# Joint block products for six shared chunks of batches 0 and 1, and the mixed weights of both batches on GpSimd

## The chip, the cores and the metric

The kernel runs on one core of a Trainium2 chip. The metric is the device time of one execution in microseconds. Engine names in the profile: PE is TensorE's matmul side and PEld its weight load, DVE is VectorE, ACT is ScalarE, POOL is GpSimd, SP is the engine that issues most DMAs.

## The reference

Four layers follow one another, each added to its input, for x of 4 batches x 512 rows x 256 columns, all in fp32:

```
x = x + shared_mlp(x) + sum over the 2 best of 8 experts of share * skill_mlp(x)   # gelu(x@gate) * (x@up) @ down, inner width 1024
x = x + (silu(x@Wu.T + bu) * (x@Wg.T + bg)) @ Wd.T + bd                            # one expert of 8, inner width 512
x = x + x @ (sum_g y[b,g] * weight[g] * mask).T + bias                             # mixed weights, 256 x 256
x = x + x @ W_base.T + b_base + 2 * lora(x)                                        # low rank, mixed by y[b]
```

The experts of the first two layers and the shares y[b] come from `cond_8`, one row for each batch. The shared MLP of the first layer is the same for all batches, the skill MLPs are chosen for each batch.

## The kernel before

Inner width is worked off in chunks of 128. The first layer has 8 shared chunks and 2 x 8 skill chunks for each batch, the second has 4. A chunk is: gate and up products (12 matmuls of 512 columns), gelu on ScalarE into `hid`, the product with up on VectorE (`hidden`, L966 to L970), and a down product (6 matmuls). Each fp32 operand is split into a high half (fp32r, made by ScalarE: `hid_hi`, `w_hi`) and a low half (the rest, made by VectorE: `hidden_lo` L976, `split` L956), and each product is three matmuls: high x high, high x low, low x high. The weights of two chunks come as one piece of four DMAs into one of three `raw` slots; SP issues them in a fixed order and waits for the splits of the piece three earlier.

Every engine's order is written out by hand. TensorE interleaves: gate and up of chunk i, then down of chunk i-1. VectorE in a chunk does `hidden`, the low half of the weights of chunk i+2 (`split`), `hidden_lo`, and then what the tables at the top of the file name for this chunk: turning x or the second layer's weights, summing `a2` (the mixed weights of the third layer, 8 steps of `a2_step_n`, L1022 to L1031), bias sums (`bias_base`, L1202 to L1207), residual sums.

Batches 0 and 1 run one after the other through `batch`, 24 chunks each, the 8 shared ones first. Batches 2 and 3 share their 8 shared chunks: `pair_head` does 8 skill chunks of batch 2, then 8 calls of `pair_unit` do one skill chunk of batch 2 and one shared chunk of both batches, then `pair_rest` does batch 3's 16 skill chunks. In a unit the gate and up of the shared chunk, for two batches, would be 8 block products of three matmuls; seven are done, on sums of the x blocks (`t_tiles`, made once) and sums of the weight blocks (`pair_sums` L1374 to L1379, `pair_main_lo` L1386, `pair_sums_lo` L1391), and their results are put together by VectorE (L1405, L1418, L1431) and ScalarE copies. TensorE's products 0 to 6 of a unit are lines L1825 to L1827; the second waits for the last sum (L1431) of the unit before, the down product after it for `hidden_lo` (L976) of the unit's own skill chunk.

At the start, TensorE turns batch 0's x and sums the routing result (`route`, L1787); VectorE's `take_route` (L1157, L1160) writes the chosen experts, for which SP waits before any skill piece. Pieces 1 and 2 are of the shared MLP and are issued before that wait.

Of the kernel before, what the change touches and what calls it, by code (L numbers as in the profile page):

```python
# [5 lines left out]
F32 = mybir.dt.float32  # L6
# [9 lines left out]
E = 8  # L16
# [6 lines left out]
CH = 3 * MLP_CHUNKS  # L23
C1 = H1 // P
PIECES = CH // 2
# [10 lines left out]
MINE_AT = 3  # L36
X_TURN_AT = {4: 1, 7: 2, 9: 3}
X_HI_AT = {5: 1, 8: 2, 10: 3}
X_LO_AT = {6: 1, 9: 2, 12: 3}
L3_TURN_AT = 6  # L40
L3_OPERAND_AT = 7
L3_HI_AT = 8
BIAS_BASE_AT = 1
BIAS_LORA_AT = 2
BIAS_AT = 3
BIAS_LOADS_AT = 18
L3_LO_AT = 10
L1_AFTER = 5
X2_AT = L1_AFTER + 1
OUT_AT = 8  # L50
C_AT = 13
CA_AT = CH - 1
XSUM_AT = 14
TURN_AT = 15
# [3 lines left out]
C_PLACE = {2: 1, 3: 3}  # L58
OUT_PLACE = {2: 7}
X2_SUM = {2: 5}  # L60
# [3 lines left out]
CA_PLACE = 13  # L64
A_HEAD = {1: (0, 1), 2: (2, 3), 3: (4, 5), 4: (7,), 6: (8,), 7: (9,)}
A_BESIDE_L1 = 6
PAIR_SUMS_AT = 4
PAIR_SUMS_LO_AT = 5
X1_PLACE = 2
# [7 lines left out]
def first(b):  # L77
    return isinstance(b, int) and b == 0

def a_steps_at(b, i):  # L80

    if not first(b):
        return (i - 9,) if 9 <= i <= E + 10 else ()
    return {13: (0,), 14: (1, 2)}.get(i, (i - 12,) if 15 <= i <= E + 13 else ())

def a_split_at(b):
    return E + 14 if first(b) else E + 11

PAIR = 2
SKILL = 2 * MLP_CHUNKS  # L90
L1_PLACE = {1: 5, 2: 3, 3: SKILL}
X2_PLACE = {2: 4}
HIDDENS = [0, CH, 2 * CH + C1, 2 * CH + SKILL + 2 * C1, 2 * CH + 2 * SKILL + 2 * C1]
PAIR_FROM = HIDDENS[PAIR] + MLP_CHUNKS + C1
PAIR_TO = HIDDENS[PAIR + 1]
PRODUCTS, COPIES, SUMS, PARTS = 7, 3, 4, 3
# [5 lines left out]

def tile_of(g):
    return g % 2 if g < PAIR_FROM else 1 if g < PAIR_TO else (g + 1) % 2


def same_tile_before(g):

    return g - 1 if PAIR_FROM <= g <= PAIR_TO else g - 2


def splits_done(b, i):
    return min(b, PAIR) * (CH - 2) + (2 + (b - PAIR) * SKILL if b >= PAIR else 0) + i + 1

# [4 lines left out]

def tails_before(b):  # L120
    return b * 3 - 1 + len(PREPS) if not first(b) else len(PREPS)


def hidden_of(b, i):
    return i + (0 if first(b) or i <= L1_PLACE[b] else C1)


def turned(i):
    c, odd = divmod(i - TURN_AT, 2)
    return c if 0 <= c < C1 and not odd else None  # L130
# [6 lines left out]
def product_of(b, what):  # L137
    order = ("c", "ca", "out") if b > PAIR else ("c", "out", "ca") if b == PAIR else ("out", "c", "ca")
    return order.index(what) + 1 - first(b)


def raw_slot(p):
    return (p - 1) % RAW_SLOTS if p else RAW_SLOTS - 1


def raw_uses(b, p):

    s = raw_slot(p)
    per = sum(raw_slot(q) == s for q in range(1, PIECES))
    return per * b + sum(raw_slot(q) == s for q in range(1, p + 1))  # L150


PAIR_PIECES = [("skill", 0), ("skill", 2), ("skill", 4), ("pair", 0), ("skill", 6), ("skill", 8), ("pair", 2), ("skill", 10),
               ("pair", 4), ("skill", 12), ("pair", 6), ("skill", 14)] + [("skill", SKILL + c) for c in range(0, SKILL, 2)]


def pair_raw_slot(j):
    return (j + 2) % RAW_SLOTS


def pair_raw_uses(j):
    return raw_uses(1, (9, 10, 11)[j % RAW_SLOTS]) + j // RAW_SLOTS + 1


X_LAST = 4 * PAIR + KD


def piece_of(kind, c):
    return PAIR_PIECES.index((kind, c - c % 2))


def build(nc, t):
    ctx = ExitStack()
    with ctx:
# [3 lines left out]
        def sem(name):  # L178
# [54 lines left out]
        base_nat = sums[:, :, :].rearrange("p (k n) m -> p k (n m)", k=KD)  # L233
# [10 lines left out]
                    3: xs[:, :, :].rearrange("p k s -> p (k s)")}  # L244
# [93 lines left out]
        a2_step = sem("a2_step")  # L338
        weights_f = sem("weights_f")
# [61 lines left out]
        t_tiles = (out_pair[:, 0], sums_flat, c3[:, :], out_pair[:, 1])  # L401
# [22 lines left out]
        PHASE = [(res_hi, res_lo, n) for n in range(2)] + [(w_hi, w_lo, n) for n in range(2, W_SLOTS)]  # L424
        AFTER_PAIR = [(res_hi, res_lo, 0), (w_hi, w_lo, 0)] + [(w_hi, w_lo, 2), (w_hi, w_lo, 3), (res_hi, res_lo, 0), (res_hi, res_lo, 1)] * 4

        def split_slots(i, b=0):
# [5 lines left out]
            if i < 2:  # L433
                return res_hi[:, i], res_lo[:, i]
# [1539 lines left out]
```

## Time and profile before

| | us |
|---|---|
| time, median of 3 runs (483.36 to 483.56) | 483.42 |
| span of the profiled execution | 481.8 |
| PE busy | 477.8 |
| DVE busy | 374.9 |
| ACT busy | 262.7 |
| POOL busy | 33.7 |

The page gives the profiled execution's own time as its span, from the first to the last instruction. The timed runs last 1.6 us longer than the span. Busy times are unions of instruction intervals; those of PE contain its weight waits within the pipeline, so a pace is better read from the distance of two starts.

### The profile page before, as it was taken

To read this page: it belongs to the slowest core of one execution; us is meant where nothing else is said; L and a number is where in the kernel's file an instruction comes from. 1 tells how busy PE (TensorE), PEld (TensorE's weight loads), DVE (VectorE), ACT (ScalarE), POOL (GpSimd) and SP (SyncE) were. 2 spreads that over 40 slices of the span, in tenths; PEclk is the share of its full clock that TensorE was granted. 3 is DMA by queue.
4 is the path that set the end of the run, shared out by engine and by line. 5 is a ranking of instruction groups with operands and counts; after the bars stand their busy time and mean duration, and the time that the engine had idled before them with its cause. 6 is when DMAs were issued, how large, how long until landed. Compare 5 with 4: busy or idle time off the path is not lost.

```text
span 481.8 us, 6729 instructions
## 1 busy us (share of the span) xinstructions
PE 477.8 (99%) x2184; PEld 398.5 (83%) x2184; DVE 374.9 (78%) x642; ACT 262.7 (55%) x418; POOL 33.7 (7%) x56
## 2 busy tenths in 40 slices
PE   9999999999999999999999999999999999999997
PEld 7888888888888888888888888888888888888886
DVE  7678989969536578985988988998887799965465
ACT  5556555545446344555547566676765365544432
POOL 1910302000100200000000020000000100000000
PEclk9999999999999999999999999999999999999999
DMA  7988985386230532424290053404059224000002
GB/s 224 199 184 201 261 168 153 71 195 134 70 106 0 136 106 67 131 67 131 78 180 4 2 149 93 131 1 131 0 117 205 74 66 128 4 1 0 2 0 87
DMA packets 114538, 48.90 MB, mean 101 GB/s; under 512 B 66552, under 2 KB 113272, under 8 KB 114504
## 3 DMA queue, kind: packets, MB, share of 16 engines
q1 hardware_dynamic: 111360, 42.88, 35.9%
q0 software_dynamic: 2560, 5.21, 4.5%
q10 hardware_dynamic: 584, 0.39, 0.3%
q8 instruction: 17, 0.28, 0.3%
q14 instruction: 17, 0.14, 0.1%
HBM read 46.36 MB, written 2.10 MB: 101 GB/s over the span
## 4 chain that ended last, share of the span: by engine, by line
PE 99%; DVE 0%; DVEq 0%; issue 0%
PE bank_a L1568 9%; PE bank_a L1569 9%; PE bank_b L1569 9%; PE bank_a L1570 9%; PE bank_b L1570 9%; PE bank_b L1568 9%; PE out L1593 6%; PE out L1596 6%; PE out L1592 6%; PE tail L1593 2%; PE tail L1596 2%; PE tail L1592 2%; PE tail L1570 2%; PE tail L1569 2%; PE tail L1568 2%; PE bank_a L1825 2%
## 5 line engine op out<-in xcount | busy, mean ns | idle before, releaser
L706 ACT ACTIVATE hid_hi<-hid 128x512 fp32r<-128x512 f32 x96 | 60.7, 632 | 93.2 <-DVE hid L968 54.0
L976 DVE TENSOR_TENSOR hid_lo<-hid,hid_hi 128x512 fp32r<-128x512 f32 x96 | 66.0, 687 | 16.8 <-ACT hid_hi L706 16.8
L698 ACT ACTIVATE hid<-bank_a 128x512 f32<-128x512 f32 x80 | 47.7, 596 | 55.1 <-PE bank_a L1570 54.3
L968 DVE SCALAR_TENSOR_TENSOR hid<-bank_b,mine,hid 128x512 f32<-128x512 f32 x64 | 47.7, 746 | 32.8 <-PE bank_b L1570 30.6
L956 DVE TENSOR_TENSOR w_lo<-raw,w_hi 128x768 fp32r<-128x768 f32 x57 | 54.1, 949 | 0.4 <-ACT w_hi L665 0.4
L1568 PE MATMUL bank_a<-x_hi,w_hi 128*128 128x512 f32 x114 | 44.5, 391 | 0.0
L1569 PE MATMUL bank_a<-x_lo,w_hi 128*128 128x512 f32 x114 | 44.5, 390 | 0.0
L1570 PE MATMUL bank_a<-x_hi,w_lo 128*128 128x512 f32 x114 | 44.4, 390 | 0.0
L1570 PE MATMUL bank_b<-x_hi,w_lo 128*128 128x512 f32 x114 | 44.4, 389 | 0.0
L1569 PE MATMUL bank_b<-x_lo,w_hi 128*128 128x512 f32 x114 | 44.4, 389 | 0.0
L1568 PE MATMUL bank_b<-x_hi,w_hi 128*128 128x512 f32 x114 | 44.4, 389 | 0.0
L1593 PE MATMUL out<-hid_hi,w_lo 128*128 128x512 f32 x104 | 40.5, 389 | 0.0
L1592 PE MATMUL out<-hid_hi,w_hi 128*128 128x512 f32 x104 | 40.5, 389 | 0.0
L665 ACT ACTIVATE w_hi<-raw 128x768 fp32r<-128x768 f32 x44 | 36.9, 838 | 0.2 <-DMA raw<-in_L_cond_shared_down 0.2
L1596 PE MATMUL out<-hid_lo,w_hi 128*128 128x512 f32 x104 | 32.0, 389 | 0.0
L1568 PEld LDWEIGHTS bank_a<-x_hi,w_hi 128*128 128x128 f32 x114 | 21.4, 188 | 4.5 <-DVE w_lo L956 0.2
L1568 PEld LDWEIGHTS bank_b<-x_hi,w_hi 128*128 128x128 f32 x114 | 21.4, 188 | 4.5
L1570 PEld LDWEIGHTS bank_a<-x_hi,w_lo 128*128 128x128 f32 x114 | 21.4, 188 | 4.5
L1569 PEld LDWEIGHTS bank_b<-x_lo,w_hi 128*128 128x128 f32 x114 | 21.4, 188 | 4.4
L1570 PEld LDWEIGHTS bank_b<-x_hi,w_lo 128*128 128x128 f32 x114 | 21.4, 188 | 4.4
L1569 PEld LDWEIGHTS bank_a<-x_lo,w_hi 128*128 128x128 f32 x114 | 21.4, 188 | 4.2
L1593 PEld LDWEIGHTS out<-hid_hi,w_lo 128*128 128x128 f32 x104 | 19.5, 188 | 4.0
(346 smaller groups left out, 1108.9 us busy)
## 6 DMA issues: line engine op xcount, KB each, us to landing
raw<-in_L_cond_skill_gate SPq DMA_DIRECT2D x32, 256.0 KB, 3.0
raw<-in_L_cond_skill_up SPq DMA_DIRECT2D x32, 256.0 KB, 3.2
raw<-in_L_cond_skill_down SPq DMA_DIRECT2D x64, 128.0 KB, 3.3
raw<-in_L_cond_shared_down SPq DMA_DIRECT2D x22, 128.0 KB, 3.8
raw<-in_L_cond_shared_gate SPq DMA_DIRECT2D x10, 256.0 KB, 3.6
raw<-in_L_cond_shared_up SPq DMA_DIRECT2D x10, 256.0 KB, 3.7
raw_gate<-in_L_cond_W_gate SPq DMA_DIRECT2D x16, 128.0 KB, 3.0
early<-in_L_cond_weight POOLq DMA_DIRECT2D x2, 1024.0 KB, 7.6
```

Of the source, the lines that this page charges most:

```text
L665: nc.scalar.activation(split_slots(i)[0], raw[:, raw_slot(p), :, (i % 2) * P:(i % 2 + 1) * P], ACT.Copy).then_inc(split_hi, 1)
L698: nc.scalar.activation(hid[:, tile_of(g)], bank_a[tile_of(g)][:, :], func, **kw).then_inc(act_ready, 1)
L706: nc.scalar.activation(hid_hi[:, tile_of(g)], hid[:, tile_of(g)], ACT.Copy).then_inc(hid_hi_ready, 1)
L956: nc.vector.tensor_tensor(lo, raw[:, slot, :, (i % 2) * P:(i % 2 + 1) * P], hi.bitcast(F32), ALU.subtract).then_inc(split_lo, 1)
L968: ins = nc.vector.scalar_tensor_tensor(tile, bank, weight, tile, ALU.mult, ALU.mult)
L976: nc.vector.tensor_tensor(hid_lo[:, tile], hid[:, tile], hid_hi[:, tile].bitcast(F32), ALU.subtract).then_inc(hid_lo_ready, 1)
L1568: nc.tensor.matmul(out, w_hi_, v_hi, start=start, stop=False)
L1569: nc.tensor.matmul(out, w_hi_, v_lo, start=False, stop=False)
L1570: return nc.tensor.matmul(out, w_lo_, v_hi, start=False, stop=stop)
L1592: nc.tensor.matmul(banks[:, j, :], hi[:, 4 + j], hid_hi[:, tile], start=start, stop=False)
L1593: nc.tensor.matmul(banks[:, j, :], lo[:, 4 + j], hid_hi[:, tile], start=False, stop=False)
L1596: ins = nc.tensor.matmul(banks[:, j, :], hi[:, 4 + j], hid_lo[:, tile], start=False, stop=stop)
```

## The change

Batches 0 and 1 get the joint stage that 2 and 3 have, for six of the eight shared chunks. Each of the two now starts with 2 shared chunks of its own (`SHARED`). `first_head` does 12 chunks of batch 0 (2 shared, 10 skill), six units do the last 6 skill chunks of batch 0 beside six joint chunks, `second` does 18 chunks of batch 1 with the second layer's four chunks after chunk 4. The functions of the joint stage take the batch as an argument; banks and tiles of batch 0's units are those with number 0.

Beside that:
- The piece after the first one is a skill piece; SP waits for `chosen_ready` ahead of it. `take_route` is cut in two: `take_chosen` is done right after the first part of the first weights, `take_picks` where `take_route` stood.
- x of batches 2 and 3 is loaded and turned in batch 1 instead of batch 0; combined x tiles of batches 0 and 1 are made in chunks 5 to 10 of batch 0.
- The `a2` steps of batches 0 and 1 are done by GpSimd (`first_a2`), in its queue between DMAs; the first waits for `bias_base`, which VectorE now does in unit 0. Those of batches 2 and 3 stay on VectorE.
- The second layer's weights of batch 0 are turned in units 1 to 4, those of batch 1 in its chunks 13 to 16, one chunk each time.
- Placement tables of bias sums, c3 and ca products follow. Sums of batch b go to bank `out0` or `tail` by the parity of b.

```diff
-L1_PLACE = {1: 5, 2: 3, 3: SKILL}
+PAIRED = {0: 0, 2: 6}
+SHARED = 2
+OWN = (SHARED + 2 * MLP_CHUNKS, SHARED + 2 * MLP_CHUNKS, 2 * MLP_CHUNKS, 2 * MLP_CHUNKS)
+UNITS = {b: MLP_CHUNKS - c for b, c in FIRST_JOINT.items()}
+L1_PLACE = {1: 4, 2: 3, 3: OWN[3]}
+T_AT = {5: 0, 7: 1, 9: 2, 10: 3}
+MAIN_AT = 10
+SUMS_AT = {0: 10, 2: 4}
+SUMS_LO_AT = {0: 11, 2: 5}
-PAIR_TURN = {1: 0, 2: 1, 4: 2, 6: 3}
-PAIR_TURN_AT = {2: 0, 3: 1, 5: 2, 7: 3}
+PAIR_TURN = {0: {1: 0, 2: 1, 3: 2, 4: 3}, 2: {1: 0, 2: 1, 4: 2, 6: 3}}
+PAIR_TURN_AT = {0: {2: 0, 3: 1, 4: 2, 5: 3}, 2: {2: 0, 3: 1, 5: 2, 7: 3}}
+PIECE_ORDER = ([("own", 0, c) for c in range(0, 14, 2)] + [("joint", 0, 2), ("own", 0, 14), ("joint", 0, 4), ("own", 0, 16), ("joint", 0, 6)]
...
 # SP
-            load_piece(1, None, *shared)
-            load_piece(2, None, *shared)
-            load_piece(3, splits_done(0, 1), *shared)
-            load_x(1)
             sp.wait_ge(chosen_ready, 1)
+            for j, (kind, b, c) in enumerate(PIECE_ORDER):
...
 # GpSimd
+            def first_a2(b):
+                if b == 0:
+                    pool.wait_ge(base_sums, KD)
+                    pool.wait_ge(w2_in, 48)
+                    pool.wait_ge(tail_free, len(PREPS))
+                else:
+                    pool.wait_ge(weights_lo, 3 * b - 1)
+                nc.gpsimd.tensor_scalar(a2[:, :], w2_raw[:, 0, :], picks[:, b, 5:6], None, ALU.mult).then_inc(a2_step, 1)
+                for n in range(1, E):
+                    pool.wait_ge(a2_step, b * A_STEPS + n)
+                    nc.gpsimd.tensor_scalar(share, w2_raw[:, n, :], picks[:, b, 5 + n:6 + n], None, ALU.mult).then_inc(a2_share, 1)
+                    pool.wait_ge(a2_share, b * (E - 1) + n)
+                    nc.gpsimd.tensor_tensor(a2[:, :], a2[:, :], share, ALU.add).then_inc(a2_step, 1)
+                pool.wait_ge(a2_step, b * A_STEPS + E)
+                nc.gpsimd.tensor_tensor(a2[:, :], a2[:, :], mask_nat[:, :], ALU.mult).then_inc(a2_step, 1)
...
 # VectorE, first_head (12 chunks of batch 0)
+                    hidden(0, i, weight=mine[:, skill_of(0, i):skill_of(0, i) + 1] if i >= SHARED else None)
+                    if i + SPLIT_AHEAD <= UNIT_AT[0]:
+                        split(0, i + SPLIT_AHEAD)
+                    if i:
+                        hidden_lo(0, i)
...
+                    if i == SUMS_AT[0]:
+                        pair_sums(0, 0)
+                    if i == MAIN_AT + 1:
+                        pair_main_lo(0, 0)
+                    if i == SUMS_LO_AT[0]:
+                        pair_sums_lo(0, 0)
+                    if i == C_PLACE[0] + 2:
+                        weights_split_lo(0, 1, c3_hi, c3_lo, c3[:, :])
 # VectorE, pair_unit(b, m)
+                if m in PAIR_TURN[b]:
+                    turn_chunk(b, PAIR_TURN[b][m])
+                if unit == 0:
+                    bias_base()
+                hidden(b, n, weight=mine[:, 1:2])
 # VectorE, start
             first_parts(0)
+            take_chosen()
             first_x_parts(0)
...
 # TensorE
+            first_head()
+            for m in range(UNITS[0]):
+                pair_unit(0, m)
+            second()
             pair_head()
-            for m in range(MLP_CHUNKS):
-                pair_unit(m)
+            for m in range(UNITS[JOINT]):
+                pair_unit(JOINT, m)
```

## Rows read from the trace of the kernel before

**Rows 1.** Page, part 1: busy us, share of the span, instructions.
```profile
PE 477.8 (99%) x2184; PEld 398.5 (83%) x2184; DVE 374.9 (78%) x642; ACT 262.7 (55%) x418; POOL 33.7 (7%) x56
```
**Rows 2.** Page, part 4: chain that ended last, by engine.
```profile
PE 99%; DVE 0%; DVEq 0%; issue 0%
```
**Rows 3.** Chain in order of time (start us, us, what): low-half down matmuls.
```profile
21.25 0.45 PE out L1596 x2
...
57.97 0.45 PE out L1596 x2
...
103.59 0.45 PE out L1596 x2
```
**Rows 4.** Engines by stretch, one unit: length; busy us (instructions) by engine; clock, DMA.
```profile
287.90:299.46 11.56, 11.56 (x53) 9.59 (x52) 10.52 (x22) 7.75 (x14) 0.00 (x0) 1.00 0.42 130
```
**Rows 5.** Timeline at the start (start us, us, engine, line, instruction, idle before).
```profile
6.04 0.42 DVE L1534 TENSOR_TENSOR res_lo<-raw,res_hi 128x256 fp32r<-128x256 f32 x1
...
9.51 0.15 DVE L1157 CAST chosen<-out 1x12 int32<-1x12 f32 x1
...
11.35 0.85 ACT L665 ACTIVATE w_hi<-raw 128x768 fp32r<-128x768 f32 x1 [0.23 <-DMA raw<-in_L_cond_shared_down]
...
12.23 0.96 DVE L956 TENSOR_TENSOR w_lo<-raw,w_hi 128x768 fp32r<-128x768 f32 x1 [0.38 <-ACT w_hi L665]
...
13.24 0.19 PEld L1568 LDWEIGHTS bank_a<-x_hi,w_hi 128*128 128x128 f32 x1 [0.24 <-DVE w_lo L956]
```
**Rows 6.** Timeline of SP's DMA issues.
```profile
13.31 5.40 SPq L482 DMA_DIRECT2D early<-in_x  x4
20.01 0.43 SPq L448 DMA_DIRECT2D raw<-in_L_cond_skill_gate  x1
...
37.16 0.52 SPq L448 DMA_DIRECT2D raw<-in_L_cond_skill_gate  x1
...
38.38 1.39 SPq L451 DMA_DIRECT2D raw<-in_L_cond_skill_down  x2
```
**Rows 7.** Page, part 6: DMA issues, KB each, us to landing.
```profile
raw<-in_L_cond_skill_gate SPq DMA_DIRECT2D x32, 256.0 KB, 3.0
...
raw<-in_L_cond_skill_down SPq DMA_DIRECT2D x64, 128.0 KB, 3.3
```
**Rows 8.** Timeline of DVE in a chunk that has no weight split.
```profile
103.16 0.75 DVE L968 SCALAR_TENSOR_TENSOR hid<-bank_b,mine,hid 128x512 f32<-128x512 f32 x1 [0.71 <-PE bank_b L1570]
104.61 0.69 DVE L976 TENSOR_TENSOR hid_lo<-hid,hid_hi 128x512 fp32r<-128x512 f32 x1 [0.70 <-ACT hid_hi L706]
```
**Rows 9.** Groups of instructions (count, busy us, mean ns): low halves of a unit's weight blocks.
```profile
L1386 DVE TENSOR_TENSOR w_lo<-raw,w_hi 128x512 fp32r<-128x512 f32 x8 | 5.5, 686 | 0.3 <-ACT w_hi L756 0.3
```
**Rows 10.** Timeline of PE, unit 0 and the start of unit 1.
```profile
283.48 0.40 PE L1827 MATMUL bank_a<-x_hi,w_lo 128*128 128x512 f32 x1
...
288.60 0.40 PE L1825 MATMUL bank_b<-x_hi,w_hi 128*128 128x512 f32 x1
...
290.19 0.62 PE L1596 MATMUL out<-hid_lo,res_hi 128*128 128x512 f32 x2
```
**Rows 11.** Timeline of DVE in units 0 and 3.
```profile
283.92 0.69 DVE L1418 TENSOR_TENSOR xs<-bank_a,xs 128x512 f32<-128x512 f32 x1 [0.81 <-PE bank_a L1827]
...
286.67 0.69 DVE L1431 TENSOR_TENSOR xs<-bank_b,xs 128x512 f32<-128x512 f32 x1
...
288.48 0.68 DVE L976 TENSOR_TENSOR hid_lo<-hid,hid_hi 128x512 fp32r<-128x512 f32 x1
...
317.39 0.69 DVE L1418 TENSOR_TENSOR xs<-bank_a,xs 128x512 f32<-128x512 f32 x1 [0.41 <-PE bank_a L1827]
```
**Rows 12.** Timeline of DVE, bias sums in batch 1.
```profile
115.82 0.42 DVE L1202 CUSTOM_DVE_ANT_0 bias_all<-sums,bias_all 128x256 f32<-128x256 f32 x1
...
117.14 0.69 DVE L970 TENSOR_TENSOR hid<-bank_b,hid 128x512 f32<-128x512 f32 x1
```
**Rows 13.** Timeline of POOL: the only arithmetic that reads SBUF there.
```profile
1.32 0.28 POOL L581 TENSOR_SCALAR_AFFINE_SELECT ident<-ident 128x128 f32<-128x128 f32 x1 [0.23 <-POOL ident L579]
```

More of the change, by code:

```diff
@@ L554, in later_skill @@
[L554 to L565 removed]
+            sp.wait_ge(chosen_ready, 1)
@@ new lines, in _ @@
+            for j, (kind, b, c) in enumerate(PIECE_ORDER):
+                if j == 0:
+                    continue
+                own_skill = c - (SHARED if b < JOINT else 0)
+                if kind == "own" and own_skill >= 0 and own_skill % MLP_CHUNKS == 0:
+                    rows = skill_rows(b, own_skill // MLP_CHUNKS)
+                load_piece(j, *(rows if kind == "own" and own_skill >= 0 else shared))
+                if (kind, b, c) == ("own", 0, 4):
+                    load_x(1)
+                if (kind, b, c) == ("own", 0, 14):
+                    for n in range(3):
+                        first_l1(n)
+                if (kind, b, c) == ("own", 1, 2):
+                    sp.wait_ge(turn_f, 3 * C1)
+                    load_x(2)
+                    load_x(3)
+                if (kind, b, c) in (("own", 1, 12), ("own", 2, 6), ("own", 3, 2)):
+                    later_l1(b)
@@ L655, in split @@
             def split(b, i):
-                if b >= PAIR:
-                    return later_split(b, i)
-                p = i // 2
-                act.wait_ge(raw_in[raw_slot(p)], 64 * raw_uses(b, p))
-                if i - W_SLOTS >= 2:
-                    wait(act, down_done, hiddens_before(b) + hidden_of(b, i - W_SLOTS) + 1)
-                elif not first(b):
-                    last = max(c for c in range(CH) if c >= 2 and (c - i) % W_SLOTS == 0)
-                    act.wait_ge(down_done, hiddens_before(b) - CH + last + 1)
@@ L729, in l1_chunks, with combined_hi @@
                     hidden_hi(b, n0 + c)
-                    if b == PAIR:
+                    if b == 1 and c == 2:
+                        later_x_hi(2)
+                    if b == JOINT:
                         beside_l1(c)
+            def combined_hi(b, which):
+                steps = 5 * (b // JOINT)
+                for n, step in which:
+                    act.wait_ge(t_step, steps + step)
+                    nc.scalar.activation(combined(b, x_hi, n), t_tiles[b][n], ACT.Copy).then_inc(t_hi, 1)
@@ new lines, in pair_unit @@
+                if not last:
+                    pair_main_hi(b, m + 1)
+                else:
+                    split(b + 1, 0)
+                if (b, m) == (JOINT, 1):
+                    weights_split_hi(ca_hi, tail[:, 1, :], (tail_ready, tails_before(JOINT) + product_of(JOINT, "ca")))
+                act.wait_ge(pair_product, PRODUCTS * unit + 3)
+                wait(act, pair_hid_lo, 2 * unit)
+                if (b, m) == (JOINT, 0):
+                    act.wait_ge(xs_lo_ready, 4 * JOINT)
@@ L1298, in batch @@
-                    if b == 1 and i == BIAS_LORA_AT:
+                    hidden(b, n, weight=mine[:, skill_of(b, i):skill_of(b, i) + 1] if i >= SHARED else None)
+                    if i + SPLIT_AHEAD < OWN[b]:
+                        split(b, i + SPLIT_AHEAD)
+                    else:
+                        split(JOINT, i + SPLIT_AHEAD - OWN[b])
+                    hidden_lo(b, n)
+                    if i == 0:
+                        stage_mine(b)
+                        stage_bias1(b)
+                        x_sum(0)
@@ L1941, in _ @@
             route()
-            batch(0, False)
-            batch(1, True)
+            first_head()
+            for m in range(UNITS[0]):
+                pair_unit(0, m)
+            second()
             pair_head()
-            for m in range(MLP_CHUNKS):
-                pair_unit(m)
+            for m in range(UNITS[JOINT]):
+                pair_unit(JOINT, m)
             pair_rest()
```

1150 lines of the change are left out of this document (588 added, 562 removed).

## The prediction

> **What bounds the kernel now.** I read the page's busy times first, then the chain, then the distances of TensorE's starts, then the order of VectorE where the change puts new work. The busy line gives PE 99% of the span and VectorE 78% [rows 1]; the chain that ended last is PE for 99% [rows 2]. So a matmul that is taken out counts in full, and any wait given to TensorE counts in full too. The reader is to see the pace in the chain: the low-half down matmuls of chunks nine apart start at 21.25 and 57.97 [rows 3], 36.72 us for nine chunks of 18 matmuls, 4.08 a chunk and 0.2267 for a matmul of 512 columns. A unit of the present joint stage has 51 of them, and the stretch from one unit to the next is 11.56 us, which is 51 x 0.2267: no loss, although VectorE is busy 10.52 of the 11.56 [rows 4]. The clock granted there is 1.00, the upper level. The joint stage of before thus runs at TensorE's pace with VectorE close behind. The one loss after the start-up is at the third chunk, where the weight load sat idle 0.24 us for the low half of the weights [rows 5].
>
> **The sum's base.** The sum is made on the profiled span, 481.8; the timed runs are 1.6 longer (median 483.42), and that part is left as it is.
>
> **What goes.** Six units each need 7 instead of 8 block products of three matmuls: 18 matmuls x 0.2267 = 4.1 us less. No other matmul is removed or added. Fewer shared pieces are loaded, which nobody waits for. VectorE loses 16 steps of `a2`, each of the form of the 0.75 us row [rows 8], and the masks; TensorE waits for VectorE nowhere in batches 0 and 1 after the third chunk, so this gives nothing by itself: it makes room.
>
> **Start-up, third chunk.** The third chunk's weights are now those of an expert, and SP issues them only when the choice is known. VectorE makes the choice after the first weights' low half, which ends at 6.46, with a copy of 0.15 [rows 5]: about 6.6. From there to the first issue I take the gap that SP has in front of its first skill piece, 18.71 to 20.01, 1.3 us [rows 6] (register load and addresses; at least the 0.5 of an issue must pass): 7.9. The last of a piece's four DMAs starts 1.92 after the first (38.38 + 0.70 - 37.16) [rows 6]: 9.8. It lands 3.3 later [rows 7]: 13.15. Before, landing at 11.35 let the low half be ready at 13.19, 1.84 later [rows 5]; now 15.0. TensorE starts there instead of at 13.24: +1.7. From below, with 3.0 to landing and 0.5 for SP: +0.6. From above, a second start of the kind where the DMA is slower by 1 us: +2.7. The queue behind this wait is ScalarE's gelu of the second chunk, and VectorE's product; both catch up inside the 2.7 us of the third chunk's gate and up. The early copy itself delays the x parts by 0.15, inside the same wait.
>
> **Entry into unit 0.** Product 0 of unit 0 needs the low half of the main weight blocks. In the stage of before it is made in the second layer's chunks, far ahead. Here VectorE makes it in chunk 11, behind that chunk's `hidden_lo`, and TensorE needs it right after the down product of chunk 10. A chunk without a split shows the times: `hidden` starts at 103.16, `hidden_lo` at 104.61, free at about 105.22, against down matmuls whose last pair starts at 103.59 and ends its slot at 104.04 [rows 3, 8]. Chunk 10's tail (combined low halves and weight sums) makes VectorE late by 0.16 by my count. So 105.22 + 0.16 + 0.69 for the first low half [rows 9] = 106.07 against 104.04: +2.0. Below, 1.6, if the low half may start 0.4 earlier; above 2.4, if the late work of chunks 8 to 10 is not caught up.
>
> **Unit 0 into unit 1.** VectorE gets `bias_base` between its sums and `hidden`. From its first instruction to the next one behind it are 1.32 us [rows 12]. Product 1 of unit 1 waits for the last sum, which before ended at 287.36, 3.88 after the start of product 4's last matmul at 283.48 [rows 10, 11]. With 1.32 it is 5.20. In unit 0 of before the ca product lay in this stretch; now it doesn't, and the distance from that matmul to product 1 is 1 + 6 + 6 + 3 = 16 matmuls, 3.63 us (before, 288.60 - 283.48 = 5.12). So TensorE waits 1.57. The next wait is for `hidden_lo`, which ended at 289.16, 5.68 after the matmul, now 7.00; TensorE gets there at 3.63 + 1.57 + 1.59 (290.19 - 288.60) = 6.79: 0.2 more. Together +1.8, bounds 1.4 and 2.4. The next joint piece, which SP can issue only once chunk 13 is split late in unit 0, lands about 5.2 us later and would make VectorE's next weight sums wait; by then these are late by the same 1.8, so I charge it nothing (uncovered it would be 0.9).
>
> **Edits charged nothing.** Units 2 to 4 each carry a turn and the low half of the one before. The trace has one such unit, and in the next VectorE still had to wait 0.41 for TensorE at its third step [rows 11]: it fits, with 0.4 to spare each time; without the cover 3 x 0.4 at most. Loading and turning x later, the combined x tiles, `ca` of batch 0 in batch 1, the denser turns of batch 1: a chunk has 4.08 us and VectorE's own work in it is 0.75 + 0.96 + 0.69 = 2.4 [rows 5, 8]; no chunk gets over 2.4 more for longer than two chunks, and where the cover is gone it costs some tenths. SP's queue has the L1 loads ahead of the fourth joint-stage piece, but that piece waits for unit 0 anyway. The GpSimd chain starts after `bias_base`, behind the bias DMAs in its queue, and its result is wanted in chunk 1 of batch 1, more than four units of 11.56 later; behind its second part wait the bias rows, wanted in chunk 10.
>
> **GpSimd's arithmetic.** No row shows a GpSimd step of this size. Bounds: VectorE's 0.69 for 512 columns [rows 8], and four times the 0.28 of 128 columns, 1.12 [rows 13]. With 16 big steps and two small ones for each batch, 11.6 to 18.5 us. This is off the path whatever it is, unless it slows VectorE; no row of before has the two side by side, so the bounds of that are 0 and the whole 18.5 for batch 0. I take 0, since the nearest rows (VectorE's 0.69 and 0.75) never vary.
> The Trainium skill speaks against that: "SBUF — State Buffer", section "Who interferes with whom", says that a VectorE instruction with two SBUF inputs and a GpSimd instruction that reads SBUF lock each other out for a whole instruction, the one that starts first going first. Nothing in this trace shows it, and it is a rival below.
> "GPSIMD Engine Reference", section 3.1, puts a two-input fp32 step at some 2.6 cycles an element; by that a step of 512 would take an estimated 1.3 us, the chain would be about a fifth longer than my upper bound, and still early enough.
>
> **Sum.** 481.8 - 4.1 + 1.7 + 2.0 + 1.8 = 483.2, with the 1.6 around the span 484.8. The three waits give back more than the products save.
>
> **Rivals.**
> (1) GpSimd holds VectorE up. Its 18 steps of batch 0 begin at the end of unit 0 and fall in units 1 to 3, where VectorE has 1 us to spare in 11.56 [rows 4]. 14 of a unit's 19 or so VectorE instructions read two tiles in SBUF. If each GpSimd step catches one of them half done, VectorE loses 18 x 0.5 x 1.03 = 9, less 2 of slack: TensorE +7. In batch 1 the 1.7 us a chunk swallow it. Time 491; up to 500 if each step is lost whole. For it: that VectorE's spare time is so small just there. Against it: DMA issues on GpSimd lie beside unchanged VectorE rows.
> This is the skill's rule named above.
> (2) On the other side: the new joint stage runs as the old one does, and only the start costs. Place: the border of chunk 11 and unit 0, and `bias_base` in unit 0. Price: 3.8 less, 481.0. It decides for this if the main low half is there within 1.4 us of the beginning of chunk 10's down product, or if the last sum of unit 0 comes within 3.6 of product 4. For it: the 11.56 of each old unit. Against it: the written orders and rows 8 to 12.
> (3) Only one of the two joint-stage waits shows, because the first shifts TensorE against work that VectorE has already done: 482.9, no change.
>
> **How the numbers follow.** The forecast, 484.8 with its own range 483.6 to 486.4, gets 0.47; rival 1 gets 0.28 (487 to 500), rival 2 0.14, rival 3 0.11. The measurement can't tell less than 0.2%, 1.0 us: same is 482.4 to 484.4. Faster: rival 2 and a little of rival 3, 0.16. Same: most of rival 3 and the lower part of the forecast, 0.22. Slower: 0.62. The range 482.4 to 495 leaves out rival 2 and the upper part of rival 1, 0.2 together.
>
> **What would show it.** PE instructions 18 fewer; the third chunk's first weight load at about 15.0 with an idle time near 2 before it, released by w_lo; an idle of 2 in front of the first L1825 product of batch 0's unit 0, released by the low half from raw; one of 1.6 in front of product 1 of unit 1, released by VectorE's last sum, and 0.2 at the down product behind it. All other units at 11.56. VectorE's rows of 512 columns at 0.69 and 0.75 beside GpSimd's steps would refute rival 1; longer ones, or gaps between them, in units 1 to 3 would show it. The prediction is wrong if unit 0 starts on time, if the granted clock falls behind one of the waits, or if batch 1 shows waits of its own.

## The result and the profile after

| | before | after |
|---|---|---|
| median | 483.49 us (483.36 to 483.69, 4 runs) | 492.92 us (492.59 to 494.70, 4 runs) |
| profiled execution: own time, span | 483.42, 481.8 | 492.72, 491.1 |
| ratio to before | | 1.0189, 95% interval 1.0159 to 1.0220 |

Forecast 484.8, range 482.4 to 495: the sign and the range hold, the likeliest case was 8.1 us too low. The measured time lies outside the forecast's own interval (483.6 to 486.4) and inside that of rival 1 (487 to 500).

The page of the kernel after, its busy line, then the clock line of its slices and the chain by engine [rows 1, 2]:
```profile
PE 476.2 (97%) x2166; PEld 393.8 (80%) x2166; DVE 398.1 (81%) x679; ACT 274.6 (56%) x448; POOL 89.4 (18%) x92
...
PEclk9999999999999999999999999999999999999999
...
PE 82%; DVE 8%; SPq 5%; DMA 3%; issue 1%; ACT 0%; ACTq 0%; DVEq 0%
```
18 matmuls fewer, as worked out. But PE is busy 1.6 us less in a span 9.3 longer, and the chain that was TensorE for 99% now has VectorE, SP's queue and a transfer in it. VectorE is busy longer than before (398.1 against 374.9 us), although its 16 steps of 0.75 us for the mixed matrices of batches 0 and 1 are gone.

TensorE's longest waits in the kernel after (what waited, for whom; us in total, times, longest):
```profile
PE bank_b L1938 <- DVE xs L1533: 3.5, 2, 1.9
PE bank_a L1671 <- DVE w_lo L995: 2.3, 1, 2.3
PE bank_a L1938 <- DVE w_lo L1485: 1.9, 1, 1.9
PE bank_a L1938 <- ACT xs L813: 1.5, 1, 1.5
PE out L1699 <- DVE hid_lo L1014: 1.4, 2, 1.2
```
A wait is told only up to the release; what a matmul loses shows better in the distances between starts. I took the distance from each TensorE start to the next, less 0.2267 for each 512-column matmul between them, and summed what is over 0.03 us. Before 4.2 us, after 17.4: 13.2 more, less 4.1 for the products is 9.1, against 9.3 in the span. Where it lies (us; "clock" is the part lost where matmuls stand 0.43 apart instead of 0.23; the start, the same within 0.3 us in these profiles but for e8's clock, is left out; the other kernels of the table come below):

| profile | third chunk | entry unit 0 | entry unit 1 | middle unit 1 | unit 2 | unit 3 | batch 1 | clock |
|---|---|---|---|---|---|---|---|---|
| before | 0.1 | - | - | - | - | - | 0 | 0 |
| after | 2.5 | 2.2 | 3.6 | 1.8 | 0.5 | 2.4 | 0 | 0 |
| e7, batch 0's weights on VectorE | 1.7 | 2.3 | 1.9 | 3.0 | 0 | 0.2 | 2.5 | 2.6 |
| e8, all four repairs | 0 | 0.8 | 0.6 | 0 | 0 | 0 | 2.5 | 1.8 |
| e9, and an earlier split | 2.5 | 0.8 | 0.6 | 0.5 | 0 | 0 | 0.3 | 0 |

e8's 0 and 1.8 belong together: its first chunks ran at the pace of the lower clock, and by their end the third chunk's weights were there. The rows of e8 and e9 at the entry into unit 0 take in what is lost inside that unit.

TensorE and VectorE of the kernel after at these places (timeline: start us, us, engine, line, instruction, idle time before and its releaser):
```profile
15.85 0.19 PEld L1671 LDWEIGHTS bank_a<-x_hi,w_hi 128*128 128x128 f32 x1 [2.70 <-DVE w_lo L995]
...
59.62 0.50 PE L1938 MATMUL bank_a<-x_hi,w_hi 128*128 128x512 f32 x1 [1.92 <-DVE w_lo L1485]
...
71.34 0.50 PE L1938 MATMUL bank_b<-x_hi,w_hi 128*128 128x512 f32 x1 [1.51 <-DVE xs L1533]
...
74.44 0.73 PE L1699 MATMUL out<-hid_lo,res_hi 128*128 128x512 f32 x2 [1.22 <-DVE hid_lo L1014]
...
79.42 0.50 PE L1938 MATMUL bank_a<-x_hi,w_hi 128*128 128x512 f32 x1 [1.52 <-ACT xs L813]
```
The first answers to the last of [rows 5] (0.24), the others have no counterpart before. The next timeline puts GpSimd's first steps of the kernel after beside VectorE's instructions of the same time, which follow in the second fence:
```profile
72.52 1.32 POOL L622 TENSOR_TENSOR a<-a,base_nat 128x512 f32<-128x512 f32 x1
...
79.09 1.67 POOL L622 TENSOR_TENSOR a<-a,base_nat 128x512 f32<-128x512 f32 x1
...
94.59 1.62 POOL L624 TENSOR_TENSOR a<-a,mask_nat 128x512 f32<-128x512 f32 x1
```
VectorE:
```profile
72.62 1.76 DVE L1014 TENSOR_TENSOR hid_lo<-hid,hid_hi 128x512 fp32r<-128x512 f32 x1
...
77.95 0.32 DVE L1473 TENSOR_TENSOR sums<-raw 128x128 f32<-128x128 f32 x1 [1.76 <-DMA raw<-in_L_cond_shared_down]
...
78.92 2.12 DVE L1485 TENSOR_TENSOR w_lo<-raw,w_hi 128x512 fp32r<-128x512 f32 x2
...
94.98 2.04 DVE L995 TENSOR_TENSOR res_lo<-raw,res_hi 128x768 fp32r<-128x768 f32 x1
```
`hid_lo` starts 0.1 behind the GpSimd step, and ends 0.54 after that step's end at 73.84, as if it had done almost nothing until then: its length of before is 0.69 [rows 8]. L995 at 94.98 ends 0.81 after the mask's end at 96.21. The row at 77.95 is of another kind: a transfer that wasn't there.

Two theories: A, GpSimd's reads of SBUF stop VectorE, which has 1 us to spare in a unit, and these losses are the larger part; B, the waits come from the orders written for VectorE and SP, and the long rows are a side effect. A can't be all of it: the waits at 12.97 and 57.08 lie ahead of GpSimd's first arithmetic (69.21), and at 77.5 VectorE itself had stood idle for a transfer.

### The profile page after: what moved, and what is told of

Read it like the earlier page. It is cut to its first block, busy times and chain, and to the rows that moved or that the text cites. A ratio compares the mean times of both kernels' runs of the same rounds, so it can differ in the third digit from the quotient of the medians.

```text
span 491.1 us, 6836 instructions
## 1 busy us (share of the span) xinstructions
PE 476.2 (97%) x2166; PEld 393.8 (80%) x2166; DVE 398.1 (81%) x679; ACT 274.6 (56%) x448; POOL 89.4 (18%) x92
## 4 chain that ended last, share of the span: by engine, by line
PE 82%; DVE 8%; SPq 5%; DMA 3%; issue 1%; ACT 0%; ACTq 0%; DVEq 0%
PE bank_a L1671 7%; PE bank_b L1673 7%; PE bank_b L1671 7%; PE bank_a L1673 7%; PE bank_a L1672 7%; PE bank_b L1672 7%; PE tail L1695 4%; PE tail L1696 4%; PE tail L1699 4%; SPq L496 3%; PE out L1699 3%; PE out L1695 3%; PE out L1696 3%; PE bank_a L1938 2%; PE bank_a L1940 2%; PE bank_a L1939 2%
## 5 line engine op out<-in xcount | busy, mean ns | idle before, releaser
L995 DVE TENSOR_TENSOR res_lo<-raw,res_hi 128x768 fp32r<-128x768 f32 x36 | 36.1, 1004 | 1.1 <-ACT res_hi L692 1.1
L995 DVE TENSOR_TENSOR w_lo<-raw,w_hi 128x768 fp32r<-128x768 f32 x30 | 29.5, 984 | 2.8 <-ACT w_hi L692 2.8
L692 ACT ACTIVATE res_hi<-raw 128x768 fp32r<-128x768 f32 x36 | 30.2, 839 | 1.2 <-DMA raw<-in_L_cond_skill_down 1.2
L1671 PE MATMUL bank_a<-x_hi,res_hi 128*128 128x512 f32 x74 | 28.9, 390 | 0.0
L1672 PE MATMUL bank_a<-x_lo,res_hi 128*128 128x512 f32 x74 | 28.8, 390 | 0.0
L1673 PE MATMUL bank_a<-x_hi,res_lo 128*128 128x512 f32 x74 | 28.8, 389 | 0.0
L1671 PE MATMUL bank_b<-x_hi,res_hi 128*128 128x512 f32 x74 | 28.8, 389 | 0.0
L1673 PE MATMUL bank_b<-x_hi,res_lo 128*128 128x512 f32 x74 | 28.8, 389 | 0.0
L1672 PE MATMUL bank_b<-x_lo,res_hi 128*128 128x512 f32 x74 | 28.8, 389 | 0.0
L620 POOL TENSOR_SCALAR base_nat<-early,picks 128x512 f32<-128x512 f32 x14 | 26.1, 1863 | 1.4
```

Source lines behind the costliest of these rows:

```text
L692: nc.scalar.activation(split_slots(b, i)[0], own_raw(b, i), ACT.Copy).then_inc(split_hi, 1)
L995: nc.vector.tensor_tensor(lo, own_raw(b, i), hi.bitcast(F32), ALU.subtract).then_inc(split_lo, 1)
L1671: nc.tensor.matmul(out, w_hi_, v_hi, start=start, stop=False)
L1672: nc.tensor.matmul(out, w_hi_, v_lo, start=False, stop=False)
L1673: return nc.tensor.matmul(out, w_lo_, v_hi, start=False, stop=stop)
```

## The experiments

Every time is the median of its runs, in us, with the ratio to the kernel before on the same chip and its 95% interval. The ratio is made from all runs of both kernels, so it isn't the quotient of two medians; the kernel before had medians of 483.6 to 483.8 on these chips. The code lines are shortened cuts.

**e1, GpSimd only writes.**
```
-nc.gpsimd.tensor_scalar(a2[:, :], w2_raw[:, 0, :], picks[:, b, 5:6], None, ALU.mult).then_inc(a2_step, 1)
+nc.gpsimd.memset(a2[:, :], 0.0).then_inc(a2_step, 1)
```


> The changed kernel, but GpSimd's twenty steps for the second layer's mixed weights of each pair (L617 to L628) are memsets of the same tiles: GpSimd writes and no longer reads, in the same order and with the same semaphores. The mixed weights are zeros in this run. Theory A (GpSimd's reads hold VectorE up in the joint stage: eviction L1262 0.57 instead of 0.16, L1014 at 72.62 taking 1.76 instead of 0.69, the halves L995, L1485 taking 2.0 instead of 0.95): the stretched VectorE rows go back to their own lengths, the 2.4 us lost at the entry into unit 2 and about 1.8 of the 3.6 at the entry into unit 1 go, and the time is 488.0 to 489.5. Rival B (the joint stage waits because of its own order; the long VectorE rows are waits of another kind): 492.9, same waits as before. What stays in either case: 2.5 at the third chunk, 2.2 at the entry into unit 0, 1.8 in the middle of unit 1.


Measured 492.62 (487.10 to 493.14, 6 runs), 1.0131 (1.0087 to 1.0174). By the median theory A fails; the trace says otherwise. VectorE's rows beside the writes (timeline, same instructions):
```profile
70.92 0.16 DVE L1262 TENSOR_TENSOR base_b<-base_b,base_sum 128x2 f32<-128x2 f32 x1
...
73.58 0.69 DVE L1014 TENSOR_TENSOR hid_lo<-hid,hid_hi 128x512 fp32r<-128x512 f32 x1
...
79.47 0.29 DVE L1473 TENSOR_TENSOR sums<-raw 128x128 f32<-128x128 f32 x1 [3.12 <-DMA raw<-in_L_cond_shared_down]
```
0.16 and 0.69 are back, and VectorE is busy for 387.2 us in place of 398.1 with the same 679 instructions; entry into unit 1 loses 1.9 instead of 3.6, unit 2 0, unit 3 0.2: 4.4 us of waits gone. Two things ate them. The transfer that VectorE awaits in the middle of unit 1 came at its own time, so an earlier VectorE only waits longer (3.4 instead of 1.8). And the granted clock fell twice, for about 3.4 us each, after the wait at the third chunk and after that of unit 1. The engines in these two stretches (busy us and count by engine; clock behind POOL):
```profile
16.60:20.00 3.40, 3.40 (x10) 2.63 (x9) 1.38 (x3) 1.75 (x3) 3.40 (x7) 0.51 1.32 154
81.50:85.00 3.50, 3.50 (x10) 2.74 (x9) 2.84 (x6) 1.62 (x3) 0.00 (x0) 0.51 0.04 11
```
TensorE's rows at the first of them:
```profile
15.81 0.50 PE L1671 MATMUL bank_a<-x_hi,w_hi 128*128 128x512 f32 x1 [2.03 <-DVE w_lo L995]
...
16.97 0.63 PE L1672 MATMUL bank_a<-x_lo,w_hi 128*128 128x512 f32 x1
17.39 0.63 PE L1673 MATMUL bank_a<-x_hi,w_lo 128*128 128x512 f32 x1
17.82 0.63 PE L1671 MATMUL bank_b<-x_hi,w_hi 128*128 128x512 f32 x1
```
0.51 is the lower of the two levels, 1.2 GHz; the starts stand 0.43 apart. That cost 3.0 us. The one run of this kernel with mean clock 1.00 took 487.1, 5.6 less than the kernel after at 1.00 (492.72); the account above gives 2.8 of that (4.4 less 1.6), and the rest has no trace to explain it. So A holds for where VectorE's time went, and what it costs in the end depends on the other waits.

**e2, e3, e11: the kernel before with idle GpSimd put to work.** All are beside batch 2's joint units, whose pace of before is 11.56 [rows 4], and nobody uses the result. e2:
```
+nc.gpsimd.tensor_scalar(beside, w2_raw[:, m, :], picks[:, b, 5 + m:6 + m], None, ALU.mult)
+nc.gpsimd.tensor_tensor(beside, beside, w2_raw[:, m, :], ALU.add)      # 9 of each, in turn
```


> The kernel before, nothing of the change in it; GpSimd is given 18 steps of 128x512 (9 TENSOR_SCALAR, 9 TENSOR_TENSOR, all reading the raw second-layer weights) whose result nobody reads, placed behind the bias loads of the third batch, about 284 to 315, beside the joint units of batches 2 and 3, which run at pace (11.56 per unit) in the kernel before. Theory A (reads of GpSimd hold VectorE up): the VectorE rows of that stretch get longer (0.69 to between 1.2 and 2.0 for many), TensorE loses 2 to 6 us there, 485.5 to 489.5. Rival B: TensorE keeps its pace, 483.4 to 483.7.


Measured 490.84 (489.78 to 492.02, 6 runs), 1.0135 (1.0107 to 1.0163): more than expected. In its profile the clock fell at 316.4 as well, behind a wait of 2.2; that is up to 1.9 of the 6.3 us by which the span is longer. e3 has `nc.gpsimd.memset(beside, 0.0)` sixty times in this place:


> The kernel before with 60 GpSimd memsets of 128x512 in the place of the 18 reading steps of the run beside it: GpSimd is busy in the same stretch but only writes. If it is the reads that hold VectorE up: 483.4 to 483.8. If any work on GpSimd does: as the run with the reads, 485.5 or more.


Measured 483.71 (483.34 to 486.08, 10 runs), 0.9995 (0.9972 to 1.0018). e11 has 18 of the TENSOR_SCALAR above and no TENSOR_TENSOR:


> The kernel before with 18 GpSimd steps of 128x512 in the stretch from 284 as in the earlier run, but all of them TENSOR_SCALAR, with one SBUF tile read each; their result is read by nobody. If only GpSimd's two-input steps hold VectorE up (in the earlier run each long VectorE row lies beside a GpSimd TENSOR_TENSOR, and those beside a TENSOR_SCALAR keep 0.68): 483.4 to 484.0 and VectorE's rows unchanged. If every GpSimd read does: 487 to 492, as the earlier run (490.8).


Measured 483.90 (483.74 to 486.09, 12 runs), 1.0008 (0.9991 to 1.0025). The same 34 us of the four kernels, in the order before, e2, e3, e11 (length; PE, PEld, DVE, ACT, POOL; clock, DMA):
```profile
284.00:318.00 34.00, 34.00 (x157) 28.39 (x156) 31.01 (x61) 23.65 (x43) 0.09 (x1) 1.00 0.40 117
```
Next:
```profile
284.00:318.00 34.00, 31.01 (x135) 24.13 (x134) 33.70 (x49) 18.60 (x33) 31.93 (x19) 0.98 0.40 117
```
Next:
```profile
284.00:318.00 34.00, 34.00 (x157) 28.41 (x156) 31.03 (x61) 23.70 (x43) 30.72 (x59) 1.00 0.40 117
```
Next:
```profile
284.00:318.00 34.00, 33.94 (x155) 27.83 (x154) 32.95 (x60) 23.36 (x43) 31.99 (x17) 1.00 0.40 117
```
GpSimd is busy for 30.7 to 32 us in all three. Writing costs VectorE nothing (31.03 against 31.01, with the same count). One-input reads cost it 2 us more busy time, which the spare time holds. With two-input steps in turn it is saturated (33.70) and gets through 12 instructions fewer; TensorE loses 22 matmuls (three or four of them to the clock). How one step does it, in e2, GpSimd ahead and VectorE behind:
```profile
285.75 1.87 POOL L658 TENSOR_SCALAR beside<-early,picks 128x512 f32<-128x512 f32 x1
287.70 1.50 POOL L660 TENSOR_TENSOR beside<-beside,early 128x512 f32<-128x512 f32 x1
```
VectorE:
```profile
286.76 0.67 DVE L1446 TENSOR_TENSOR xs<-bank_b,xs 128x512 f32<-128x512 f32 x1
287.36 0.67 DVE L1449 SCALAR_TENSOR_TENSOR c<-xs,c 128x512 f32<-128x512 f32 x1
287.96 1.78 DVE L1451 SCALAR_TENSOR_TENSOR xs<-xs,hid 128x512 f32<-128x512 f32 x1
```
Two VectorE steps begin beside the TENSOR_SCALAR and keep their length; the one that meets the TENSOR_TENSOR waits for its end. In e11 a TENSOR_SCALAR stands at that place, and L1451 keeps its length beside it:
```profile
287.62 2.28 POOL L660 TENSOR_SCALAR beside<-early,picks 128x512 f32<-128x512 f32 x1
```
VectorE in e11:
```profile
287.88 0.68 DVE L1451 SCALAR_TENSOR_TENSOR xs<-xs,hid 128x512 f32<-128x512 f32 x1
288.48 1.10 DVE L989 TENSOR_TENSOR hid_lo<-hid,hid_hi 128x512 fp32r<-128x512 f32 x1
```
This is theory A with nothing of the change in it, and the cause is narrower than "GpSimd reads": most of it is the steps with two SBUF inputs, seven sums and a mask for each matrix. It is narrower on VectorE's side too. Steps of VectorE that take one input from TensorE's results (a bank or `tail`), and so only one from SBUF, pass even beside a TENSOR_TENSOR. e2 again:
```profile
295.57 1.29 POOL L660 TENSOR_TENSOR beside<-beside,early 128x512 f32<-128x512 f32 x1
```
VectorE:
```profile
295.62 0.67 DVE L1058 TENSOR_TENSOR ca_lo<-tail,ca_hi 128x512 fp32r<-128x512 f32 x1
296.22 0.67 DVE L1433 TENSOR_TENSOR xs<-bank_a,xs 128x512 f32<-128x512 f32 x1
```
L989 above, 0.42 longer than its 0.68, is as far as a one-input step reaches. Of the VectorE steps that began while a TENSOR_TENSOR of 512 columns ran (more than 0.1 us before its end), those with both inputs in SBUF were longer without exception (8 in e2, 11 in the kernel after, by 0.3 to 1.1 us), those with one never (4 and 6).

The Trainium skill, "SBUF — State Buffer", section "Who interferes with whom", says that a VectorE instruction with two SBUF inputs and a GpSimd instruction that reads SBUF shut each other out for a whole instruction. The rows of the two-input steps agree; those of e11 don't go so far (the longest VectorE row of 512 columns there in the first unit is 1.10, against 0.69). It also says that a GpSimd instruction that only writes doesn't contend with such a VectorE instruction; e1 and e3 agree (0.69, and 31.03 us busy against 31.01).

**e4, the main low half of unit 0 one chunk earlier.**
```
-                    if i == MAIN_AT + 1:
+                    if i == MAIN_AT:
                         pair_main_lo(0, 0)
```


> The changed kernel with one VectorE call moved: the main product's low half of unit 0 (L1354) is made one chunk earlier, ahead of the hidden of chunk 11 instead of behind it. If the 2.1 us at the entry into unit 0 (57.08 to 59.62) is the wait for this call's place in VectorE's order, the wait goes and nothing behind takes it: 490.8. Rival: the wait goes to what is behind it on VectorE (the x_sum, the hidden of chunk 11, or the entry into unit 1), and the time stays at 492.4 to 492.9.


Measured 493.56 (491.92 to 494.66, 6 runs), 1.0178 (1.0151 to 1.0206). A miss in time, a hit in the mechanism: unit 0 enters at 59.11, 0.57 behind the start of the down pair (2.54 in the kernel after). With two small waits inside the unit 0.9 of the 2.2 us stays; nothing else took the rest. But in the profiled execution the clock fell twice again (at the third chunk and at 101), 2.8 us.

**e5, the first expert piece doesn't wait for the choice.**
```
+                if j == 1:
+                    load_piece(j, *[w[0:1].rearrange("a r c -> (a r) c") for w in skill])
+                    sp.wait_ge(chosen_ready, 1)
```


> The changed kernel, but the third and fourth chunks of batch 0 read the weights of expert 0 at a fixed address, issued before the wait for the choice (their numbers are then those of another expert). If the 2.5 us before the third chunk (12.97 to 15.85) is SP's wait for the choice, the piece is issued at about 5.3 instead of 7.7, the wait goes back to the 0.3 of the kernel before, and the time falls by 2.2 to about 490.7, or by up to 3.9 in those executions where TensorE's granted clock fell after this wait (about 16.5 to 19.9 in two traces, matmuls 0.43 apart instead of 0.23). Rival: the address or the reading of another tensor makes the transfer slow, and the wait stays, 492.9.


Measured 491.20 (489.73 to 492.59, 6 runs), 1.0144 (1.0119 to 1.0168). Issued at 5.28 instead of 7.73; the third chunk starts 0.48 behind the down pair, with no loss. It is the choice. The profiled execution is one of the slow ones of the six (492.51): the clock fell in it behind the waits at unit 0 and unit 3, 3.2 us.

**e6, W_up behind the joint piece.**
```
-                    for n in range(3):
-                        first_l1(n)
+                    first_l1(0)
+                    first_l1(1)
+                if (kind, b, c) == ("joint", 0, 4):
+                    first_l1(2)
```


> The changed kernel with the last of the three L1 loads on SP's queue (W_up, issued 68.0 to 71.3) behind the joint piece that follows, instead of ahead of it. Theory: the piece lands 3 us earlier (77.95 becomes about 75), VectorE's idle 1.76 and TensorE's 1.8 at 77.5 to 79.4 go, 491.1. Rival: GpSimd's hold on VectorE fills the gap and VectorE is as late at the next border, 492.5 to 492.9; or the turn of unit 1 now waits for W_up, slower than 492.9.


Measured 492.02 (490.95 to 494.35, 5 runs), 1.0152 (1.0128 to 1.0176). The 1.8 in the middle of unit 1 are 0.1, and units 2 and 3 lose 0.9 more than in the kernel after: half the gain goes to the rival. In the kernel after VectorE stood waiting at 76 to 78; here it meets GpSimd's steps there (L1475 at 78.67 takes 1.38 instead of 0.28). The profile is of the slowest of the five runs (494.35), with the clock falling once.

**e7, batch 0's mixed weights on VectorE, in batch 1.**
```
+A_SECOND = {0: (0,), 1: (1,), 3: (2,)}
+A_L1 = {0: (3, 4, 5), 1: (6,), 2: (7,), 3: (8, 9)}      # a2_step_n(0, n) behind these chunks
-A_SPLIT_AT = {1: 0, 13: 1}
+A_SPLIT_AT = {5: 0, 13: 1}
```


> The changed kernel with the mixed weights of batch 0 back on VectorE, ten steps spread over the first chunks of batch 1 (where it has room), and only those of batch 1 on GpSimd (after the bias rows). GpSimd is then free of arithmetic in the whole joint stage, as in the run in which it only wrote, and the result is complete. If GpSimd's reads are the cause: 487.0 to 489.0, with TensorE's losses at 72.8, 88 and 98 gone, and batch 1 without waits. Rival: the ten steps make batch 1 late, 490 or more.


Measured 493.33 (490.26 to 495.35, 6 runs), 1.0177 (1.0142 to 1.0211). Units 2 and 3 are clean and the entry into unit 1 loses 1.9, as in e1. The time isn't better: the piece still lands at 76.4 (3.0 lost); the split for batch 0's `ca` product, which is done in batch 1, is late by 2.5, as the rival had it; and the clock fell twice (2.6).

**e8, all four:** e7, e4, e6, and `bias_base` in the last joint unit instead of the first.


> All four repairs that leave the result complete: mixed weights of batch 0 on VectorE in batch 1, the main low half one chunk earlier, W_up behind the joint piece, and bias_base in the last joint unit instead of the first. If these are all causes of the losses in the joint stage, it runs at 11.56 a unit, only the 2.2 at the third chunk stays, and the time is 483.4 - 4.1 + 2.2 = 481.5 (483.2 where the granted clock falls after that wait). Rival: waits come back one after the other as VectorE has no room in units 1 to 4; 483.5 or more, no better than the kernel before.


Measured 486.44 (485.29 to 490.01, 9 runs), 1.0060 (1.0036 to 1.0084). The joint stage loses 1.4 us in place of 10.5. Left are the 2.5 in front of the `ca` product at 172.4, and some 2 at the start, where matmuls stand 0.43 apart until 10.8. The clock didn't fall there: the trace has no row of the granted clock before 10.77 (in the kernel after the rows begin at 4.72), so it hadn't yet come up. The time expected, 481.5, was missed by 4.9.

**e9, the split of that product's weights ahead of the second residual.**
```
+                    if i == A_FIRST_SPLIT:
+                        weights_split_lo(0, 2, a2_hi, a2_lo, a2[:, :])
```
ScalarE's high half is moved in the same way.


> The run with all four repairs, and the split of batch 0's mixed weights put ahead of the second residual in chunk 5 of batch 1 instead of behind it (the run before lost 2.35 us at 172.4 to 175.2, in front of the product that needs this split). Theory: that wait goes, nothing else changes: 2.4 less than its profiled 485.5, thus 483.0 (the clock fell there from 7.3 to 10.8 as well; where it doesn't, 481.8). Rival: the second residual, now 0.7 later, holds TensorE instead, 484 or more.


Measured 484.24 (482.51 to 485.96, 12 runs), 0.9998 (0.9977 to 1.0019): no difference from before that can be told. Its waits:
```profile
PE bank_a L1679 <- DVE w_lo L997: 2.2, 1, 2.2
PE out L2053 <- DVE hid L1623: 1.2, 1, 1.2
PE bank_a L1946 <- ACT xs L813: 0.2, 1, 0.2
```
The second stands in the start of every kernel here. The first is the third chunk (2.4); with the small losses of the joint stage (1.9) it is what eats the 4.1.

**e10, the piece's down parts issued from GpSimd's queue.**
```
+            for half_n in range(2):
+                pool.dma_start(raw[:, raw_slot(1), 4:6, half_n * P:(half_n + 1) * P],
```


> The run beside it, and the two down transfers of the first expert piece are issued by GpSimd's queue instead of SP's, at the same time as SP issues gate and up. Theory: the piece is complete about 1.1 us earlier (SP's issues took 7.73 to 10.08, of them 1.34 for the down parts), the third chunk starts 1.1 earlier, 481.9. Rival: what decides is the time from issue to landing with all queues busy at the start, no gain, 483.0.


Measured 486.74 (484.81 to 488.75, 12 runs), 1.0058 (1.0038 to 1.0079): 2.5 slower than e9. ScalarE's first copy of the piece began at 14.83, with the transfer as its releaser, against 13.73 in e9. The edit didn't bring the issues forward: GpSimd issued the two at 8.63 and 9.47, SP in e9 at 8.58 and 9.37. What changed is the time to landing, 5.27 us each in place of 3.23 and 4.33. Why isn't settled (SP's next piece was issued 0.95 earlier beside them), and whether an earlier issue would help wasn't tested. In this profile the clock came up late, at 10.3, which cost 1.6 us and makes up for a part of the wait behind it; the mean clock was under 1.00 in 8 of its 12 runs, and in 3 of e9's.

**e12, four shared chunks ahead and four joint ones.**
```
-SHARED = 2
+SHARED = 4
```


> The run with the repairs and the early split, but batch 0 begins with four shared chunks of its own instead of two (batch 1 too), and only four shared chunks are made jointly: the joint stage has four units. The first expert piece is then wanted two chunks (8 us) later, after the choice is long known. Fewer matmuls than before: 4 units x 3 = 12, 2.7 us less (instead of 4.1); the 2.35 in front of the third chunk goes back to 0.1 to 0.3; of the small losses of the joint stage in that run (about 2.2 in six units) some 1.6 stay. 483.45 - 2.7 + 1.6 = 482.3, faster than both kernels, and with fewer executions in which the granted clock falls. Rival: the turns, now one in each of the four units, make VectorE late at each border and the time is 483.5 or more.


Measured 489.32 (489.01 to 491.28, 6 runs), 1.0121 (1.0098 to 1.0143). The third chunk has no wait, but TensorE stands 3.5 us at the entry into unit 0 (72.8 to 76.7): I had left W_up ahead of the first joint piece on SP's queue, and that landed at 75.05, VectorE idle 3.84 for it. The fault of e6 over again, by my hand; with the piece ahead of W_up it wasn't tried. The entry into unit 1 lost 1.6 more, and the start 2.2, as the clock came up late (10.4). The hope of fewer runs with a lower clock failed: the mean was under 1.00 in five of six.

## Why the prediction was right and where it fell short

The range held because it had been drawn to take in most of rival 1. The forecast's own mechanism, three waits from the written orders, gives 484.8 together with the products; two effects that it charged nothing, GpSimd's and that of SP's queue, cost 6.2 us. That the time lies inside the range says little for the sum.

- **Products, -4.1.** Right: 2166 matmuls, 18 fewer.
- **Third chunk, +1.7 (bounds 0.6 and 2.7).** Measured +2.4, inside. The first issue was forecast at 7.9 and came at 7.73. The term that was short is the landing: I took 3.3 from the median of the profile's page [rows 7]. Three of the piece's four transfers took that (3.1 to 3.4), the last took 4.4, from 9.53 to 13.94, with the next piece issued right behind it. The kernel before shows the same for its second piece (last transfer 7.05 to 11.32, 4.3); a median hides it. e5 shows that the wait is the choice.
- **Entry into unit 0, +2.0.** Measured +2.2, released by the half and from the place named. e4 shows it. The 0.2 is a reading: [rows 3] are rows of the chain, which begins a piece where the matmul before it ends, 0.16 later than the start in the timeline (103.43 for the last pair, and 103.88 for what follows it). With 103.88 for 104.04 the sum gives 2.2.
- **Entry into unit 1, +1.8.** The order's part measured alone (e1, e7) is 1.9. In the kernel after it is 3.6, the rest being GpSimd's.
- **SP's next piece, charged nothing (0.9 uncovered).** Wrong. I had SP able to issue once chunk 13 was split, and saw the L1 loads ahead in the queue, but let them go with "that piece waits for unit 0 anyway". They hold the queue to 71.3, the split was done at 68.3. 1.8 us, and up to 3.4 once VectorE is early enough (e1); e6 and e8 show it.
- **GpSimd's steps: length bounded by 0.69 and 1.12 us.** 1.57 to 2.67 for a TENSOR_SCALAR, 1.3 to 1.7 for a TENSOR_TENSOR; batch 0's chain took 29 us (69.2 to 98.5) instead of 11.6 to 18.5. The upper bound from 128 columns was no bound.
  "GPSIMD Engine Reference", section 3.1, of the Trainium skill has 2.6 cycles an element and counts at 1.2 GHz: for 512 elements an estimated 1.1 us, and not the 1.3 that the prediction made of it. The shortest rows of a two-input step, 1.29, lie 0.2 above that, so that the prediction's figure fits by luck. The one-input step was longer still, 1.57 at the least.
- **GpSimd's effect on VectorE, taken as 0.** This is the step that failed, and the largest part of the 7.9 us by which the span was missed (491.1 against 483.2): entry into unit 1 (1.7), unit 2 (0.5) and unit 3 (2.2), 4.4 us. I took the value from the nearest rows, VectorE's that never vary, though none of them had GpSimd arithmetic beside it. Rival 1 had mechanism, place and nearly the price (+7; 4.4 came, and its 491 is close since the 1.8 of SP's queue and the 0.7 of the landing stood in for the rest). Its forecast for batch 1, that the room in a chunk swallows it, holds: no loss there though L995 takes up to 1.96.
- **The clock.** Named as a thing that would make the prediction wrong. In the profiled execution of the kernel after it never fell, so it is no part of the 9.3 us; its other three runs had a mean clock of 0.993 to 0.997 and took 492.59 to 494.70, no clear cost. In later profiles with the same waits it fell in some, not in others, for 3.4 us and 1.3 to 1.7 us of loss each time. What decides isn't settled.
- Units 4 and 5, the turns, the combined tiles: at pace, as charged.

The sum with what was measured: 481.8 - 4.1 + 2.4 + 2.2 + 1.9 + 1.8 + 4.4 + 0.3 for the start = 490.7, against 491.1.

## What to carry to other kernels

Arithmetic moved to an engine that shares memory with the busy one isn't free just because the engine is idle: try its steps with two SBUF inputs beside the work of the other engine first (as e2 does in the kernel before), and put them where that engine has room or takes an input from TensorE's banks. Where a queue carries two kinds of loads, follow it in issue order by time for every piece that the new stage awaits, not only the first. For a single transfer on the path read its own landing, not the median. Where several waits of like size lie close together, the next takes over much of what one repair gives (e1 and e4 to e7 moved the median by -1.7 to +0.6, e8 and e9 by -6.5 and -8.7), so judge each by its own rows and the time by the sum of repairs.

## What the runs showed of the hardware

- A GpSimd TENSOR_TENSOR of 128x512 fp32 (two SBUF inputs) holds a VectorE step with two SBUF inputs that starts behind it until its own end: 19 of 19 such rows in e2 and the kernel after, 0.69 becoming up to 1.79. VectorE steps with one input from TensorE's banks aren't held (10 of 10 rows).
- A GpSimd TENSOR_SCALAR of that size (one SBUF tile) makes VectorE's steps at most 0.44 us longer, and is itself stretched, from 1.57 to as much as 2.84 us (e11). Sixty GpSimd writes cost VectorE nothing (e3).
- TensorE's granted clock stood at the lower level (0.50 to 0.51) for 3.4 us in ten stretches of six profiles (e1, e2, e4 to e7). Each began within a TensorE wait of 2.1 to 3.3 us or at most 1.6 us behind it. As long waits passed without a fall in the kernel after (2.4), in e9 (2.4) and in e12 (3.5).
- In e8, e10 and e12 matmuls stood 0.43 apart from the first of 512 columns on (6.7), and the rows of the granted clock, at 1.00, begin only at 10.3 to 10.8; in the ten other profiles that have such rows they begin at 4.1 to 6.5, and the second matmul of 512 columns is on pace (0.23 to 0.24 to the next). A mean clock of 1.00, which all three profiles have, doesn't exclude such a start.
- The last two transfers of the first expert piece, 128 KB each, took 3.4 and 4.4 us to land in the kernel after and 3.2 and 4.3 in e9, the last one with the next piece issued right behind it. Issued by GpSimd's queue at the same times they took 5.3 each (e10). No run separates the causes.
